# Mamba-2 scan moved ahead of the mixture-of-experts layer in one kernel: layer norm, router and time steps prepared two groups ahead inside the scan, routing by a scattered table, expert rows added into the output by DMA

## What is computed

```python
xn = layernorm(x)                                    # 2048 x 512
# Mamba-2 branch
z, xBC, dt = split(xn @ in_proj_w.T)                 # 1024, 1280 and 16 columns
dt = softplus(dt + dt_bias)
xBC = silu(conv_b + causal 4-tap conv(xBC))          # -> x: 16 heads of 64, B: 128, C: 128
# in the kernel by chunks of 128 tokens, with cs = cumsum(dt * -exp(A_log)) in a chunk:
y = (C B^T * exp(cs_l - cs_s), lower triangle) @ (x*dt)        # within the chunk
y += C @ carried_state * exp(cs);  state = state*exp(cs_last) + B^T (x*dt*exp(cs_last - cs))
y = (y + x*D_skip) * silu(z);  y = y * rsqrt(mean(y*y)) * norm_w
mamba = y @ out_proj_w.T
# experts branch
scores = xn @ w_gate_router.T;  take the 2 best of 8, softmax over the two
moe = sum over the two of p_e * (silu(xn @ gate_e) * (xn @ up_e)) @ down_e      # 192 hidden
out = x + mamba + moe
```

## Time and profile before

| what | value |
|---|---|
| median of 3 runs | 755.43 us (752.85 to 755.72) |
| profiled execution, its own time | 756.27 us |
| its span, first to last instruction | 754.5 us |
| busy: PE, DVE, ACT, POOL | 85%, 69%, 50%, 42% of the span |
| mean granted clock of TensorE | 0.937 of full speed |
| bytes moved | 96.5 MB, 128 GB/s on the mean |

### The profile page before, as it was taken

The page is one execution under the profiler, slowest core; times in us unless marked ns, Lnnn a source line. Parts: engine busy times, 40 slices in busy tenths (PEclk is TensorE's granted clock), DMA queues, the critical chain, the costliest instruction groups (busy, mean ns, idle before and its releaser), DMA issues.

```text
span 754.5 us, 13575 instructions
## 1 busy us (share of the span) xinstructions
PE 643.8 (85%) x4169; PEld 521.1 (69%) x4170; DVE 519.1 (69%) x998; ACT 379.4 (50%) x781; POOL 313.1 (42%) x284
## 2 busy tenths in 40 slices
PE   2710399999998978899999999899999899999765
PEld 1500398989897778678778778678778678777432
DVE  6677745443433675886886986886986886897353
ACT  2823134445443657765665663654654654754410
POOL 4634422222221001264564563465464456455351
PEclk9955599999999989999999999999999999999797
DMA  9992146445656142215324324224224124124120
GB/s 313 373 397 109 57 132 204 133 132 158 186 152 256 63 155 70 73 55 154 112 55 142 112 64 135 66 76 164 89 64 154 56 83 140 56 84 139 56 74 25
DMA packets 36218, 96.52 MB, mean 128 GB/s; under 512 B 5392, under 2 KB 9360, under 8 KB 34000
## 3 DMA queue, kind: packets, MB, share of 16 engines
q1 hardware_dynamic: 28448, 67.99, 26.1%
q0 software_dynamic: 7728, 28.05, 13.0%
HBM read 73.09 MB, written 22.94 MB: 127 GB/s over the span
## 4 chain that ended last, share of the span: by engine, by line
PE 51%; issue 14%; DVE 11%; POOL 11%; DMA 5%; ACT 4%; SPq 3%; POOLq 0%; DVEq 0%; ACTq 0%
PE pi L1389 17%; PE pg L906 10%; PE pd L917 6%; PE py L1662 4%; PE po L1641 4%; PE py L1669 3%; PE px L891 2%; POOL ysq L1254 2%; POOL y L1300 2%; DVE y L1524 2%; POOL xdd L1274 2%; PE pxb L1703 2%; DMA xg<-xn_d,ic 2%; DMA xn_d<-xin 2%; DVE xs L1345 2%
## 5 line engine op out<-in xcount | busy, mean ns | idle before, releaser
L1389 PE MATMUL pi<-xh,whl 128*128 128x256 f32 x1152 | 169.1, 291 | 9.3 <-ACT raw L1320 4.8
L1389 PEld LDWEIGHTS pi<-xh,whl 128*128 128x128 f32 x1152 | 150.8, 194 | 13.7 <-issue 7.4
L1345 DVE SCALAR_TENSOR_TENSOR xs<-raw,conv_w,xs 128x256 f32<-128x256 f32 x240 | 119.5, 568 | 4.9 <-ACT xs L1323 4.9
L1641 PE MATMUL po<-wo,y 128*128 128x512 f32 x256 | 114.6, 601 | 1.9 <-POOL y L1303 1.9
L1389 PE MATMUL pi<-xl,whl 128*128 128x256 f32 x576 | 93.3, 285 | 0.0
L1641 PEld LDWEIGHTS po<-wo,y 128*128 128x128 f32 x256 | 48.1, 193 | 57.3 <-issue 55.0
L1416 ACT ACTIVATE m<-m,cst 128x128 f32<-128x128 f32 x256 | 79.4, 388 | 0.5
L1389 PEld LDWEIGHTS pi<-xl,whl 128*128 128x128 f32 x576 | 79.5, 192 | 0.0
L906 PE MATMUL pg<-ew,xgh 128*128 x312 | 65.9, 354 | 0.0
L1300 POOL TENSOR_TENSOR y<-y,e 128x1024 f32<-128x1024 f32 x15 | 35.8, 2389 | 66.6 <-DVE y L1524 66.6
L1274 POOL TENSOR_TENSOR xdd<-xdt,dec 128x1024 f32<-128x1024 f32 x15 | 29.1, 1940 | 74.2 <-DVE xdt L1542 74.2
(11 more groups left out here) (180 smaller groups left out, 1211.0 us busy)
## 6 DMA issues: line engine op xcount, KB each, us to landing
m<-cs_d SPq DMA_DIRECT2D x16, 1024.0 KB, 4.7
y_d<-yo SPq DMA_DIRECT2D x39, 256.0 KB
e<-cs_d SPq DMA_DIRECT2D x32, 256.0 KB, 4.1
ew<-in_w_gu POOLq DMA_DIRECT2D x8, 768.0 KB, 16.9
xin<-in_x SPq DMA_DIRECT2D x8, 512.0 KB, 7.4
xn_d<-xin SPq DMA_DIRECT2D x8, 512.0 KB, 23.2
xt_d<-ew SPq DMA_DIRECT2D x8, 512.0 KB, 14.0
xl<-xt_d SPq DMA_DIRECT2D x8, 512.0 KB, 3.9
```

Source lines behind the costliest of these rows:

```text
L1345: dve.scalar_tensor_tensor(out=xs[par][:, b, :], in0=raw[:, b, k:k + GT], scalar=conv_w[:, b, k:k + 1], in1=xs[par][:, b, :], op0=ALU.mult ...
L1389: mm = pe.matmul(pi[n % 2][:, h, :], whl[:, n, lo, k, h * P:(h + 1) * P], xx[:, k, :], start=k3 == 0, stop=k3 == 11)
L1641: mm = pe.matmul(po[:, :], y[:, b, :], wo[:, b, :], start=b == 0, stop=b == XB - 1)
```

## The change

The order of the parts is turned round. The scan comes first, the experts last.

- There is no pass over all of x ahead. Groups 0 and 1 are normed and projected at the start. Inside the scan, in the even tile of group g, group g + 2 is prepared: DVE takes its statistics, POOL its layer norm (`layer_norm`, 9 small instructions and two on 128 x 512), PE turns it into the banks `pi` (`turn_group`, 8 transposes), ACT and DVE split it. In the odd tile come its router product (`router`, 8 matmuls), the joining of its parts (`join`), and 18 small DVE instructions for the time steps (`time_step`). `cumulate` and `rows_of` make the sums of the time steps of group g + 1. The scan has no loop, all 16 tiles are written out.
- The gathers of expert rows and `residual` leave the scan: `finish` adds x alone.
- The routing is done in tiles 12 and 13 (`choose`, `count_picks`, `place`). The list of tokens by slot is a DRAM table of 8-byte pairs (token, weight), which POOL fills with 32 indirect DMAs of 128 pairs each (`put`), spread over tiles 13 and 14, and reads back in one DMA.
- The expert weights are loaded in the last two tiles, over the projection's weights, and split there (experts 0 to 4) and in the first expert tiles (5 to 7).
- The result of an expert tile is scaled by the pairs' weights and added into `out` by an indirect DMA that accumulates (`add_rows`). Each such DMA is issued when the one before has landed.

```diff
+            for t in range(T):                      # gpsimd
+                g, c = t // 2, t % 2
+                if t < T - 1:
+                    ...
+                    pool.tensor_tensor(xdd[:, :, :, :], xdt[:, :, :, :], heads(dec, c), ALU.mult).then_inc(xdd_done, 1)
+                if t == T - 2:
+                    put(18, 22)
+                if t:
+                    sums(t - 1)
+                if t == T - 3:
+                    put(0, 6)
+                elif t == T - 2:
+                    put(22, 26)
+                if c == 0 and g + 2 < G:
+                    layer_norm(g + 2)
+                if t:
+                    factor(t - 1)
+                if t == T - 3:
+                    put(6, 10)
+                elif t == T - 2:
+                    put(26, 32)
+                    pool.wait_ge(tab_put, 16 * 2 * T)
+                    pool.dma_start(tab[:, :, :], tab_d.rearrange("(p j) c -> p j c", p=P)).then_inc(tab_in_s, 16)
...
+            def put(first, last):
+                pool.wait_ge(pairs_done, 3)
+                pool.wait_ge(tab_set, 16)
+                for n in range(first, last):
+                    pool.indirect_dma_start(tab_d, bass.IndirectOffsetOnAxis(ap=slot_row[:, n:n + 1], axis=0),
+                                            pairs[:, n, :], None).then_inc(tab_put, 16)
...
+            def add_rows(j):
+                pool.wait_ge(y_done, j + 1 + CR)
+                if j == 0:
+                    pool.wait_ge(o_out, 16 * T)
+                else:
+                    pool.wait_ge(y_out[(j - 1) % 2], 16 * ((j - 1) // 2 + 1))
+                pool.indirect_dma_start(out, bass.IndirectOffsetOnAxis(ap=tab[:, j, 0:1].bitcast(U32), axis=0),
+                                        yo[j % 2][:, :], None, compute_op=ALU.add).then_inc(y_out[j % 2], 16)
...
+            for j in range(J + 1):
+                if j + 3 < J:
+                    gather(j + 3)
+                if j:
+                    add_rows(j - 1)
```

and on ACT, for a tile's result, which gates the down product of the next tile on PE:

```diff
+            def result(j, par, r):
+                act.wait_ge(down, j + 1 + CR)
+                if not static(j, 0, 1):
+                    act.wait_ge(y_out[par], r * 16)
+                act.activation(yo[par][:, :], pd[par][:, :], ACT.Copy, scale=tab[...]).then_inc(y_done, 1)
...
+                elif g < G - 1:                     # stage() on PE: what frees a bank of pi
+                    if n == 3:
+                        pe.wait_ge(xl_done, 2 * (g + 1) + 1)
```

More of the change, by code:

```diff
@@ L262, in front @@
-        v, s, s2, acc = steps.v, steps.s, steps.s2, steps.acc
-        e8 = [over(f"rt8_{i}", [P, T, E]) for i in range(5)]
-        t1 = [over(f"rt1_{i}", [P, T]) for i in range(6)]
-        gt = over("gt", [P, E, T])
-        tiles = over("tiles", [P, E])
-        base = over("base", [P, E])
-        end = over("end", [P, E])
-        slots = over("slots", [P, 2, T])
-        EARLY_Q = -(-(over.at - first) // (2 * D * 4))
-        hi_u = over("hi_u", [P, 2 * T], U32)
-        lo_u = over("lo_u", [P, 2 * T], U32)
@@ new lines, in gpsimd @@
+            pool.wait_ge(tab_in_s, 16)
+            pool.wait_ge(pad_out, 32)
+            pool.wait_ge(in_full, NP * G)
+            for i in range(2):
+                pool.wait_ge(xn_out[i], 16 * (G // 2))
+            gather(0)
+            gather(1)
+            sums(T - 1)
+            factor(T - 1)
+            gather(2)
+            for j in range(J + 1):
[3 more added lines that the diff above has]
+                    add_rows(j - 1)
+            for i in range(2):
+                pool.wait_ge(y_out[i], 16 * ((J + 1 - i) // 2))
@@ L822, in vector @@
             dve.sem_inc(h_done, 2)
-            for i in range(2):
-                dve.sem_inc(y_out[i], 16)
             def low(j, par):
@@ new lines, in router @@
+            def router(q):
+                pe.wait_ge(xl_done, 2 * q + 2)
+                pe.wait_ge(wr_done, 1)
+                if q >= 2:
+                    pair_free(q - 1, 3)
+                elif q:
+                    pe.wait_ge(lg_done, q)
+                n = 0
+                for half in (xh[q % 2], xl[q % 2]):
+                    for k in range(KD):
+                        mm = pe.matmul(router_out(q)[0], wrs[:, k, :], half[:, k, :], start=n == 0, stop=n == 2 * KD - 1)
+                        n += 1
+                mm.then_inc(r_done, 1)
@@ new lines, in project @@
+            def project(t):
+                if t < T - 1:
+                    pe.wait_ge(ygate, t + 1)
+                need(pe, o_done, t)
+                if t == 0:
+                    pe.wait_ge(wo_done, XB)
+                for b in range(XB):
+                    if t == T - 1 and b % 4 == 0:
+                        pe.wait_ge(last_gate, b // 4 + 1)
+                    mm = pe.matmul(po[:, :], y[:, b, :], wo[:, b, :], start=b == 0, stop=b == XB - 1)
+                mm.then_inc(op, 1)
+                pe.wait_ge(tree, 3 * t + 3)
+                pe.matmul(pk_ss, ysq[:, 0, :], ones[:, :], start=True, stop=True).then_inc(ss, 1)
@@ L1717 @@
+        with nc.Block() as engines:
+            engines.sync(sync)
+            engines.gpsimd(gpsimd)
+            engines.scalar(scalar)
+            engines.vector(vector)
+            engines.tensor(tensor)
 def kernel(**inputs):
```

2399 lines of the change are left out of this document (1120 added, 1279 removed).

## The result

The changed kernel takes 848.3 us (median of 4 runs, 847.1 to 848.7) beside 754.9 us for the kernel before on the same chip: a ratio of 1.124, with a 95% interval of 1.121 to 1.127. The forecast was 762 us, and its range ended at 802. The profiled execution has a span of 846.3 us.

The account below looks back on a forecast made before the run. The prediction took PE, full in the expert tiles and nearly full in most of the scan, as the bound. Its span was 754.5 - 227 + 20 + (120 + 186 - 92.2) = 761 us, so 762 us; range 738 to 802.

Parts of the forecast that it names:

- The front: Start to C B of tile 0: 302 becomes 75 us, as no experts and only two groups of x stand ahead.
- The loop turns' gain: Tile 0 to tile 13: two turns of the hardware loop at 4.2 us are removed, -8 us.
- I take the middle, 4.4 us, and 0.1 us until POOL issues the next: Expert tiles: an accumulating DMA lands between 3.0 and 5.7 us, so 4.5 us a tile and 186 us in all.
- The third rival: Expert tiles: the accumulate is a read and then a write, 5.7 us and more a tile, +49, 811 us; chance 0.12.
- no more than 4: Expert adds: by the skill's halved rate an add takes at most 4 us, under PE's 4.18 us a tile.
- I take 4.3 us for a group: Tile 0 to tile 13: time added for each prepared group, between 2.3 and 6.0 us; +26 for six groups.
- the bound of 6.0: Prepared groups in the scan: upper limit in us for a group, with PE's added work and the late root in full.
- the 380: Tile 0 to the start of tile 13: 360 becomes 380 us with loop turns removed, group preparation and choosing added.
- So hardly any of the 45 us hides: Tiles 13 and 14: 32 puts on POOL at 1.4 us lie almost wholly on the path, within 120 us to the first expert product.
- The second rival: Tiles 13 and 14: the puts are cheap, 30 us for 45, giving 747 us; decides from 1.2 us a put; chance 0.13.
- First product to first add: Start of the experts: the first add is issued 9.9 us after the first product, two tiles and the result.
- The last 13.2 us: Issue of the last add to the end: the add lands in 4.4 us and the end takes 0.5, 4.9 us.

## Why the forecast was wrong, step by step

**Right.** The front: 77.8 for 75, none of the experts ahead of the scan. The loop turns' gain: the two waits of DVE where the loop went round are gone. The mechanism that POOL's accumulating DMAs, and not PE, set the pace of the experts was the forecast's own.

**The step that failed: "I take the middle, 4.4 us, and 0.1 us until POOL issues the next".** Half of the miss is here, +43.4 us. The path was right, a chain of adds in which each is issued behind the landing of the one before, and two terms of it were too small. The landing is 4.8, not 4.4 us: 38 x 0.4 = 15 us. From a landing to the next issue pass 0.84 us on the mean, not 0.1: 28 us. Nothing in the forecast gives the 0.1, and a row of the kernel before has the larger figure. It stands in the timeline, in the lines left out there:

```profile
535.42 1.25 POOL L1287 DMA_INDIRECT ya<-y_d,sidx  x1 [0.82 <-POOL sidx L1282]
```

The indirect DMA waits for `sidx` of POOL itself and starts 0.82 us behind its end. In the changed kernel's trace POOL's own wait instruction is over 0.04 us behind the landing, and the issue starts 0.75 us behind that in nearly all links. So it isn't the landing's signal that is slow; the time lies between POOL's wait and its issue. Where the add or write waits for ACT's result last, it starts 0.27 us behind it by the median (37 to 39 such waits in each of three kernels). Why that is shorter no run here tests. A median "to landing" holds none of this. The plain indirect write, which the forecast put at 3.0 us, is 2.7, and an accumulate takes 2.1 us more, 0.6 of them in its issue. The third rival (read, then write, 5.7 us a tile, 811 us) had the price of the interval nearly right, at a chance of 0.12. That is luck: its 5.7 us were a landing, which took 4.8.

The Trainium skill, "DMA: Bandwidth & Descriptors", section "Anatomy of one DMA", has 2.0 us plus the bytes over 436 GB/s, which is 2.6 us for the plain write: the trace agrees, with 2.7. With a second read stream for the add, the forecast's estimate by "Collectives: The Full Stack", section "The bandwidth ceiling: the fold count and why AG ≠ RS ≠ AR", was 3.2 us, and the trace has 4.8. The part that goes with the bytes, 2.0 us for 256 KB by the run with half the bytes, is over that estimate's 1.2, and the rest, 2.8 us, is over its 2.0. The forecast's "no more than 4" is worked out nowhere, and the trace is over that too.

**"I take 4.3 us for a group".** The five group periods from tile 2 to tile 12 are 63.5 to 66.7 us, beside 55.7: 7.8 to 11. The size of one term was off: two scalings of 128x512 on POOL at 2.08 us each, where the estimate had 6.3 us for the whole norm and it was 8.1 (the nine small instructions, 3.9 us, were about as estimated). And the excess did not stop at the lateness of the root, since PE's turns, the root and the low parts all stand behind that one stretch: the bound of 6.0 "in full" was taken as a sum of PE's work and one wait, and PE had three waits, two of them behind the norm. A further term was put at nothing: PE was full and at full clock in the rows of this stretch, and with the waits its granted clock fell, for 1.6 us of the group read above. With the scaling on DVE the periods are 59.6 to 60.7 us and the stretch is 382.7 us, so the 4.3 us and the 380 would have been nearly right for that kernel.

**"So hardly any of the 45 us hides".** Right in its outcome and wrong in its composition. The stretch was 114 for 120 us, but the puts are worth 13 us of it, not 45. They are 1.27 us each, not 1.4. Without them 100.7 us stay, where the forecast's other terms make 75. What it left out is DVE's queue in tile 14: the experts of the tiles and the splits of experts 0 and 1 ahead of the carry adds, for which PE waits 11.7 us in the changed kernel and 13.4 with no scatters at all. The forecast counted only the splits of experts 2 to 4. The second rival decided from 1.2 us a put; even with no put at all the stretch gave back 13 us, so it could not have given its 15.

**The ends.** First product to first add, +6.5 us: the third gather is issued behind the last root and shares the DMA engines with 2.3 MB of weights (DMA share 0.64 in that stretch). Issued early it is in time, and 5 us of this stretch are gone. The last 13.2 us, +8.3: the forecast took 0.5 us behind the last landing. In the kernel before, 4.7 us lay there already (its last store is issued 6.7 us ahead of the end and lands in 2.0 by the earlier trace rows). Of the 13.2 us 8.4 lie behind the last landing. Behind a last transfer by POOL there are 7.1 to 8.7 us where it adds and 9.8 and 10.2 where it doesn't, behind one by SP 4.7 and 6.3. What the end waits for no row says, and this stays open.

## What to carry to other kernels

Where DMAs wait for one another, price a link as issue to landing plus the time until the next issue, and look in the trace for any DMA of that kind that starts behind a wait; here this second part, 0.84 us, cost twice as much as the error in the landing. Accumulating DMAs in series suit rows that come more slowly than some 5.6 us a 256 KB block. With two destinations, and so two in flight, a block took 4.75 us here, still without the sum of the two. And before a term is said to lie bare on the path, look at the other engine that is waited for at the same point: taking out half of a 41 us term gave 9 us and all of it 13, because DVE's own queue stood right behind it.

## What the runs showed of the hardware

**An indirect accumulate against an indirect write**, both of 128 rows of 2 KB by POOL: issue 1.59 against 0.99 us, landing 4.8 against 2.7 us, 128 packets of 2 KB against 64 of 4 KB. With 1 KB rows the accumulate lands in 3.8 us with the same issue and as many packets.

**POOL and DVE in each other's way.** Timeline of POOL in the changed kernel, the carry of tile 14 and the sums of tile 15, both while DVE splits expert weights:

```profile
565.36 5.24 POOL L517 TENSOR_TENSOR carry<-carry,cd 128x1024 f32<-128x1024 f32 x1
...
593.68 3.85 POOL L469 TENSOR_TENSOR ysq<-ysq 128x512 f32<-128x512 f32 x1 [6.61 <-ACT ysq L664]
```

The same instructions take 1.94 and 1.27 us in the scan, and this very carry 1.95 in the kernel with only the scaling moved, where it comes ahead of the splits. DVE's splits end at 568.8 there, and the carry 1.8 us behind that, as if it had stood still until then. The Trainium skill, "SBUF — State Buffer", section "SBUF: two separate sides", says that DVE and GpSimd share one pair of ports, which the one that starts first holds for a whole instruction, as when DVE reads two SBUF inputs against a GpSimd instruction that reads SBUF; the trace agrees, with 5.24 for 1.94 us.

It goes the other way too. In tile 14 DVE has eight tiny instructions for the experts of the tiles, of 0.16 to 0.5 us each. In seven kernels two of them take 1.7 to 4.9 us, and each of those fourteen ends 0.02 to 0.35 us behind the end of a whole-tile instruction of POOL (`carry` or one of the y's) that ran beside it. In the kernel with only the scaling moved the comparison runs from 537.56 to 542.41, and POOL's `carry` and y from 537.82 to 542.07. In the changed kernel it took 0.46 us, and POOL was issuing scatters then.

**Stalls that move.** Tile 13 to the first product took 114.0 to 115.4 us in four of the kernels with all scatters, and 121.0 to 122.1 in the other five, whatever their edit. Four of these five have the wait of 5 us on DVE shown above, put down to a remote releaser, where this program has no other core; the fifth has one of 3.4. In all five PE then waits 18 to 19 us for the carry adds, in the four 11.7 to 13.4, and the long instructions of the paragraph above are a part of that. What the wait in tile 13 is for stays open; a difference of up to 8 us in this stretch can't be put down to an edit.
